# Attention scores in float32r, two heads side by side in TensorE's row halves

## The reference

```python
h = emb[x]
Q, K, V = (heads(wq, bq), heads(wk, bk), heads(wv, bv))
score = jnp.einsum('bhsd,bhtd->bhst', Q, K) / jnp.sqrt(jnp.float32(D_K))
attn = jax.nn.softmax(score, axis=-1)
o = jnp.einsum('bhst,bhtd->bhsd', attn, V)
o = o.transpose(0, 2, 1, 3).reshape(B, S, D_MODEL)
return o @ wo + bo
```

## Time and profile before

| | us |
|---|---|
| median of 3 runs | 3909.69 (3908.48 to 3920.23) |
| profiled execution | 3908.45 |
| its span, first to last instruction | 3906.5 |
| TensorE busy | 3578.8 (92%) |
| VectorE busy | 2969.2 (76%) |
| ScalarE busy | 2761.6 (71%) |
| GpSimd busy | 1451.6 (37%) |

### The profile page before, as it was taken

The page is one execution under the profiler, slowest core; times in us unless marked ns, Lnnn a source line. Parts: engine busy times, 40 slices in busy tenths (PEclk is TensorE's granted clock), DMA queues, the critical chain, the costliest instruction groups (busy, mean ns, idle before and its releaser), DMA issues. The chain is left out here.

```text
span 3906.5 us, 64143 instructions
## 1 busy us (share of the span) xinstructions
PE 3578.8 (92%) x20577; PEld 1947.6 (50%) x20577; DVE 2969.2 (76%) x3944; ACT 2761.6 (71%) x3830; POOL 1451.6 (37%) x1284
## 2 busy tenths in 40 slices
PE   7699999999999999945899999999999999998688
PEld 4223333223323333222577777777777677777454
DVE  5799999889989999423588888888888888889122
ACT  2246666666666666822788999889898999988133
POOL 3000000000000000000577877777777887779000
PEclk9789999999999999977999999999999999999799
DMA  5510101010101000033011111111111111111412
GB/s 140 144 47 4 42 4 42 4 42 9 38 12 33 26 19 4 5 107 114 28 44 55 60 55 55 50 49 61 55 59 57 55 55 56 52 47 55 147 70 75
DMA packets 122134, 202.72 MB, mean 52 GB/s; under 512 B 25696, under 2 KB 68736, under 8 KB 121888
## 3 DMA queue, kind: packets, MB, share of 16 engines
q1 hardware_dynamic: 101264, 173.97, 14.0%
q10 hardware_dynamic: 19088, 21.24, 1.8%
q0 software_dynamic: 1536, 4.20, 0.7%
HBM read 148.23 MB, written 50.72 MB: 51 GB/s over the span
## 5 line engine op out<-in xcount | busy, mean ns | idle before, releaser
L1047 POOL TENSOR_TENSOR m_g<-m_hs,m_cb 128x512 f32<-128x512 f32 x1024 | 1295.4, 1279 | 375.3 <-DVE m_hs L1322 371.7
L661 DVE TENSOR_REDUCE a_mx<-a_ps_m 128x1 f32<-128x512 f32 x2048 | 1311.3, 685 | 158.1 <-PE a_ps_m L520 140.5
L632 ACT ACTIVATE a_probs<-a_ps_s 128x1024 f32<-128x1024 f32 x1024 | 995.0, 1020 | 466.9 <-PE a_ps_s L557 466.3
L1322 DVE TENSOR_TENSOR_SCAN m_hs<-m_da,m_carry,m_ps_x 128x512 f32<-128x512 f32 x768 | 967.6, 1274 | 178.8 <-PE m_ps_x L1118 157.6
L1248 ACT ACTIVATE m_da<-m_delta,m_a_cur 128x512 f32<-128x512 f32 x1024 | 735.7, 719 | 102.1 <-DVE m_hs L1322 101.3
L520 PE MATMUL a_ps_m<-a_k,a_q 112*128 112x512 bf16 x2048 | 732.6, 394 | 42.2 <-DMA a_q<-q_scr 26.7
L1233 ACT ACTIVATE m_bu<-m_dut,m_bt 128x512 f32<-128x512 f32 x1024 | 732.2, 715 | 0.2
L1118 PEld LDWEIGHTS m_ps_x<-m_ident,m_bu 128*128 128x128 f32 x4096 | 489.7, 143 | 389.3 <-issue 306.9
L1118 PE MATMUL m_ps_x<-m_ident,m_bu 128*128 128x128 f32 x4096 | 630.5, 277 | 45.2 <-DVE m_hs L1322 31.3
L1130 PE MATMUL m_ps_y<-m_ident,m_g 128*128 128x128 f32 x4096 | 619.8, 274 | 12.3 <-POOL m_g L1047 12.3
L557 PE MATMUL a_ps_s<-a_q,a_k 115*128 115x512 bf16 (+1 forms) x2048 | 612.1, 381 | 1.4
(11 more groups left out here) (154 smaller groups left out, 2311.3 us busy)
## 6 DMA issues: line engine op xcount, KB each, us to landing
m_cb<-c_scr SPq DMA_DIRECT2D x128, 512.0 KB, 3.7
y_scr<-m_ysb SPq DMA_DIRECT2D x16, 1024.0 KB, 6.6
ffn_y<-y_scr SPq DMA_DIRECT2D x16, 1024.0 KB, 10.3
a_k<-k_scr SPq DMA_DIRECT2D x224, 64.0 KB, 2.2
a_q<-q_scr SPq DMA_DIRECT2D x224, 64.0 KB, 2.6
m_xn<-xn_scr SPq DMA_DIRECT2D x16, 512.0 KB, 4.9
q_scr<-p_partsq SPq DMA_DIRECT2D x24, 256.0 KB, 2.4
k_scr<-p_partsk SPq DMA_DIRECT2D x24, 256.0 KB, 2.6
```

Source lines behind the costliest of these rows:

```text
L632: nc.scalar.activation(probs[:, t % 2, 2 * half:2 * half + 2], ps_s[half][:, :, :], ACT.Exp, scale=float(DK) ** -0.5).then_inc(exped, 1)
L661: nc.vector.reduce_max(mx[:, i // NC, i % NC:i % NC + 1], bank(i), AX.X).then_inc(m_maxed, 1)
L1047: nc.gpsimd.tensor_tensor(g[:, t % NG], hs[:, t % NHS], cb[:, quarter % 2, n % CQ], ALU.mult).then_inc(g_ok, 1)
L1322: nc.vector.tensor_tensor_scan(hs[:, t % NHS, rev], da[:, t % NDA, rev], ps_x[:, t % NX, rev], carry[:, n, i:i + 1] if p else 0.0, ALU.mul ...
```

## The change

Scores are computed from float32r, with two parts of q and k (`PARTS = 2`) and three part products in 48 rows (50 with the maximum). Two heads lie in partitions 0 to 63 and 64 to 127 of `k_st` and `q_st`. ScalarE writes the high part and VectorE the low part of the projection.

In `attention`, step `t` is four items. Each item is one turned product (heads in the order 1, 0, 3, 2) and one maximum product in the other half of the rows. The turned products go round three banks (`SR = 3`) and each exponential reads one bank. The maximum products go round four banks (`MR = 4`) and each maximum on VectorE reads two. The value products are those of step `t - 2` (`LAG = 2`), behind the second item, and `probs` has four buffers (`PR = 4`). The maximum products run 84 items ahead: 64 and `4 * EARLY = 20`, one chunk and five sixteenths. The negative maximum of the next chunk is transposed at item 54 of 64 (`NEG`) and takes a turn of the three banks; ScalarE copies it twice, GpSimd makes the low part (`low`), and SP writes four transfers. At the start, 20 maximum products come first and then the 64 weight transpositions, each followed by one. The loads of a group are 24 transfers of 128 KB. A group's four chunks are written out on TensorE and no longer looped.

```diff
-PARTS = 3
-
-Q_PART = [0, 0, 1, 1, 0, 2, 1]
-K_PART = [0, 1, 0, 1, 2, 0, 2]
+HP = HG // 2
+PARTS = 2
+
+Q_PART = [0, 0, 1]
+K_PART = [0, 1, 0]
...
+        parts = [sb(f"p_parts{n}", [P, 2, PARTS, KD, CH], F32R) for n in "qk"]
...
+                        act.wait_ge(stored[a][buf], ONE + (n - buf) * 8 * PARTS)
                         for m in range(KD):
-                            nc.scalar.activation(full[a][:, m], ps_qk[a][:, m], ACT.Identity,
-                                                 bias=b_col[a][:, m:m + 1]).then_inc(full_ok[a], 1)
+                            nc.scalar.activation(parts[a][:, buf, 0, m], ps_qk[a][:, m], ACT.Identity,
+                                                 bias=b_col[a][:, m:m + 1]).then_inc(high_ok[a], 1)

...
-                        dve.wait_ge(full_ok[a], ONE + KD * n + KD)
...
-                        nc.vector.tensor_copy(part[0], full[a][:, :, :]).then_inc(step, 1)
...
-                        nc.vector.tensor_tensor(part[2], rest[:, :, :], part[1], ALU.subtract).then_inc(parts_ok[a], 1)
-                        dve.wait_ge(parts_ok[a], ONE + n + 1)
+                        for m in range(KD):
+                            dve.wait_ge(high_ok[a], ONE + KD * n + m + 1)
+                            last = nc.vector.scalar_tensor_tensor(
+                                out=parts[a][:, buf, 1, m], in0=ps_qk[a][:, m], scalar=b_col[a][:, m:m + 1],
+                                in1=parts[a][:, buf, 0, m].bitcast(FP32), op0=ALU.add, op1=ALU.subtract)
+                        last.then_inc(parts_ok[a], 1)
...
-        k_st = sb("a_k", [P, 2, HG, S], BF16)
-        q_st = sb("a_q", [P, 2, NC, HG, CH], BF16)
+        SR, MR, PR, LAG = 3, 4, 4, 2
+        k_st = sb("a_k", [P, 2, HP, S], F32R)
+        q_st = sb("a_q", [P, 2, NC, HP, CH], F32R)
         v_st = sb("a_v", [P, 2, NT, HG, VW], FP32)
...
+        probs = sb("a_probs", [P, PR, HG, CH], FP32)
...
+        BLK = NM * NC
...
-        ps_s = [pb(f"a_ps_s{i}", [P, 2, CH], FP32) for i in range(2)]
-        ps_m = pb("a_ps_m", [P, 3, CH], FP32)
+        neg_col = sb("a_neg_col", [NM, P], FP32)
+        neg_rows = sb("a_neg_rows", [NM, PARTS, P], F32R)
+        ps_s = pb("a_ps_s", [P, SR, CH], FP32)
+        ps_m = pb("a_ps_m", [P, MR, CH], FP32)
...
         w_load, w_clear, w_transpose, w_copy, w_store, w_count, w_copied, w_stored = weight_transposes(
-            nc, sem, sb, ident32, [ps_s[i // 2][:, i % 2] for i in range(4)], *weights)
...
-
-
-        AHEAD = 2
-        NEG = 15
-        ITEMS = BLK + 1
-        def item(i):
+        EARLY = 5
+        ITEMS = HG * NT
+        HEADS = [1, 0, 3, 2]
+        NEG = 54
+        OPS = 2 * (BLK // MR)
+        W_AFTER = BLK + HG * EARLY - w_count
+        W_NEG = w_count - HG * (EARLY - 2)
+        def slot(i):
             return i if i < NEG else i + 1
-        def bank(i):
-            return ps_m[:, item(i) % 3]
-        ps_n = ps_m[0:PARTS * NM, NEG % 3].bitcast(BF16)[:, 0:P]
+        def turned(i):
+            return ps_s[:, slot(i) % SR]
+        def maxed(r, b):
+            return 2 * r + b // 2 + 1
+        ps_n = ps_s[0:NM, NEG % SR, 0:P]
...
-                        dst = q_st[KQ + i:KQ + i + 1, buf, bass.ds(c, 1)].rearrange("a c h (s n) -> a (c h s) n", n=P)
-                        sp.dma_start(dst, neg_rows[i * NM:(i + 1) * NM, :]).then_inc(neg_in, 16)
-                    sp.wait_ge(neg_in, ONE + 16 * PARTS * (m + 1))
+                    for r in range(2):
+                        for i in range(PARTS):
+                            row = r * (P // 2) + KQ + i
+                            dst = q_st[row:row + 1, buf, bass.ds(c, 1)].bitcast(FP32).rearrange("a c h (s n) -> a (c h s) n", n=P)
+                            sp.dma_start(dst, neg_rows[r * NM // 2:(r + 1) * NM // 2, i].bitcast(FP32)).then_inc(neg_in, 16)
+                    sp.wait_ge(neg_in, ONE + 32 * PARTS * (m + 1))
                     sp.nop(nofuse=True)
...
+                def low(m):
+                    pool.wait_ge(neg_h, ONE + m + 1)
                     pool.nop(nofuse=True)
-                    nc.gpsimd.tensor_copy(neg_parts[:, 0], neg[:, :]).then_inc(neg_step, 1)
-                    pool.wait_ge(neg_step, ONE + m * 3 + 1)
-                    nc.gpsimd.tensor_tensor(neg_rest[:, :], neg[:, :], neg_parts[:, 0], ALU.subtract).then_inc(neg_step, 1)
...
+                def max_free(m, i):
+                    r, b = divmod(i, MR)
+                    if r or not isinstance(m, int) or m:
+                        pe.wait_ge(m_maxed, ONE + m * OPS + maxed(r - 1, b))
+                def max_score(buf, c, i):
+                    pair, st, tc, half = i // 32, i // 8 % 4, i // 2 % 4, i % 2
+                    row = half * (P // 2)
+                    nc.tensor.matmul(ps_m[:, i % MR], q_st[row:row + KQ, buf, c, pair, st * P:(st + 1) * P],
+                                     k_st[row:row + KQ, buf, pair, tc * CH:(tc + 1) * CH],
+                                     start=True, stop=True).then_inc(m_scored, 1)
+                def max_blocks(m, buf, c, first, end, loads):
                     for i in range(first, end):
+                        if i % 32 < 2 and loads is not None:
+                            pe.wait_ge(loaded[buf][2 * (i // 32) + i % 2], ONE + loads)
+                        max_free(m, i)
+                        max_score(buf, c, i)
...
+                def turned_free(e, i, with_neg):
+
+                    q = slot(i) - SR
+                    if q >= 0:
+                        if q == NEG and with_neg:
+                            pe.wait_ge(neg_h, ONE + e + 2)
                         else:
+                            pe.wait_ge(exped, ONE + e * ITEMS + (q if q <= NEG else q - 1) + (q != NEG))
+                    elif not isinstance(e, int) or e:
+                        pe.wait_ge(exped, ONE + e * ITEMS + min(0, q + 2))
...
+                def turned_score(buf, c, t, h):
+
+                    row = h % 2 * (P // 2)
+                    nc.tensor.matmul(turned(HG * t + HEADS.index(h)), k_st[row:row + KQM, buf, h // 2, t * P:(t + 1) * P],
+                                     q_st[row:row + KQM, buf, c, h // 2], start=True, stop=True).then_inc(scored, 1)
...
                         last = nc.tensor.matmul(ps_o[h * VW:(h + 1) * VW, :], v_st[:, buf, t, h],
-                                                probs[:, t % 2, h], start=t == 0, stop=t == NT - 1)
+                                                probs[:, t % PR, h], start=t == 0, stop=t == NT - 1)
                     last.then_inc(pv_done, 1)
...
+                    pe.wait_ge(neg_in, ONE + 32 * PARTS * (e + 1))
...
                     for t in range(NT):
-                        maximum()
-                            for i in range(2):
-                                last = nc.tensor.matmul(ps_s[half][:, i], k_st[0:KQM, buf, 2 * half + i, t * P:(t + 1) * P],
-                                                        q_st[0:KQM, buf, bass.ds(c, 1), 2 * half + i].rearrange("p c n -> p (c n)"),
-                                                        start=True, stop=True)
-                                if i == half:
-                                    maximum()
-                        if with_neg and t == 3:
-                            if m_buf is None:
-                                transpose_neg(e + 1, G * NC * BLK + 2)
-                            else:
-                                transpose_neg(e + 1, (e + AHEAD) * BLK + NEG)
-                        maximum()
-                        if t > 0 or v_buf is not None:
-                            pe.wait_ge(exped, ONE + e * NT * 2 + t * 2 + 2)
-                            if t == 1:
-                                pe.wait_ge(o_copied, ONE + e)
-                            values(v_buf if t == 0 else buf, (t - 1) % NT)
-
+                        block, ahead = (first, 1) if t + EARLY < NT else (second, 2)
+                        for j in range(HG):
+                            i = HG * t + j
+                            m = (i + HG * EARLY) % BLK
+                            if i == NEG and with_neg:
+                                pe.wait_ge(exped, ONE + e * ITEMS + NEG - SR + 1)
+                                transpose_neg(e + 1)
+                            if block is not None:
+                                m_buf, m_c = block
+                                if m_buf != buf and m_c == 0 and m % 32 < 2:
+                                    pe.wait_ge(loaded[m_buf][2 * (m // 32) + m % 2], ONE + loads)
+                                max_free(e + ahead, m)
+                            turned_free(e, i, with_neg)
+                            turned_score(buf, c, t, HEADS[j])
+                            if block is not None:
+                                max_score(m_buf, m_c, m)
+                            if j == 1 and (t >= LAG or v_buf is not None):
+                                pe.wait_ge(exped, ONE + e * ITEMS + HG * (t - LAG + 1))
```

(51 more changed lines are left out.)

168 lines of the change are left out of this document (47 added, 121 removed).

## The result

The changed kernel took 3878.4 us (median of six runs, 3866.3 to 3894.6) beside 3910.0 for the kernel before: a ratio of 0.9916 with a 95% interval of 0.9889 to 0.9944. The interval leaves out 1, but the gain is under 1%. The direction was right and the size was not: 32 us came instead of 168. Its profiled execution took 3872.7 (span 3870.8) against 3908.45.

The account below looks back on a forecast made before the run. TensorE's 2.84 us step bounded attention; the ring of three banks would make it 2.43, a chunk 40.2, and attention 1306 against 1455 (-149). With the start's -17, 3908.45 becomes 3742 us, range 3655 to 3830.

Parts of the forecast that it names:

- One pass, row halves side by side, the ring and not an engine decides: Attention's score products: float32r takes one pass, both row halves overlap, and the ring of three banks sets the step.
- VectorE's 2.27: Attention step: two maxima of two banks at a pace of 1.13 take VectorE 2.27 us, lower bound of the step.
- I put a pair at 0.22 (0.30 at most, if two loads of 0.14 do not hide): TensorE in attention: two products in the two row halves, with their float32r weight loads, are issued in 0.22 us.
- the ring's wait: Three score banks: a product waits 1.11 us behind that of three places earlier, 0.47 to the reader, 0.60 and 0.04.
- the forecast's 2.43: Attention step: ring wait 1.11, pair 0.22 and value block 1.10 make 2.43 us, bounds 2.27 and 2.56.
- The chunk's extras, 1.3: Each attention chunk: output copy, two maxima copies, a transposition and the ring's start add 1.3 us, bounds 0.6 and 2.5.
- The chain of the maxima "just fits", charged 0: Chunk's start: transposition, copies and transfers of the maxima take 5.3 us, ten pairs last about 5.7; 0 charged.
- 18 us are left for loop returns and both ends: Attention before the change: what remains of 1455.3 us after thirty chunks (1371) and the last two (67), left unchanged.
- The start, 0.67 an item: Attention's start: 64 weight transpositions, each with a maximum product, 0.67 us each, bounds 0.57 and 0.85, 43 us.
- Stores, 7.6 us uncovered: Attention's start: ScalarE's eight stores of transposed weights, formerly under running maxima, put 7.6 us ahead of the first exponential.
- Rival (e): Attention: the clock falls to half because pairs leave TensorE less busy, a tile about 3.7, +400 us; chance 0.04.
- Rival (b): Attention: the neg chain is late or pairs take 0.30, 41.6 to 43 a chunk, 3787 to 3831; chance 0.18.

Follow-up runs that it names:

- run 2: Changed kernel with exponentials over only 256 of each bank's 512 columns, the other half of the probabilities left at one: 3779.3 us.
- run 3: Changed kernel with each maximum on VectorE reading 256 of each bank's 512 columns, so maxima over half the keys: 3869.7 us.
- run 10: Changed kernel with the column maxima transposed at item 60 of a chunk's 64 instead of 54, 1.5 steps later: 4042.2 us.
- run 5: Changed kernel with attention's start in rounds of four weight transpositions, then four maximum products, instead of one and one in turns: 3870.1 us.
- run 8: Changed kernel, still float32r, with value block in two 256-column blocks, start in rounds of four, unread products in the last steps, stores from SP: 3768.1 us, 0.9636 of before.
- run 1: Changed kernel with two bf16 parts instead of two float32r parts, in the same rows, banks and order: 3749.3 us.
- run 7: Changed kernel with each of the 64 weight transpositions of attention's start issued twice: 3884.6 us.
- run 6: Changed kernel with unread products of the maximum's shape in the other row half during the last 21 steps: 3872.6 us.
- run 4: Changed kernel with each step's value block in two blocks of 256 columns, one behind each two items: 3791.6 us, 0.9688 of before.
- run 9: Changed kernel in bf16 parts, with value block in two 256-column blocks, start in rounds of four, weight stores from SP: 3648.4 us, 0.9321 of before.

## Why the prediction failed, by its own steps

- **One pass, row halves side by side, the ring and not an engine decides**: right, by the pair's two starts and by runs 2 and 3. VectorE's 2.27 is close behind, as run 2 shows.
- **"I put a pair at 0.22 (0.30 at most, if two loads of 0.14 do not hide)"**: the failed step, 92 of the 131 us. The doubt written there was right and its size was not. The two float32r loads of a pair start together and last 0.185 each, beside a pass of 0.21, and a pair takes 0.34. Ahead of the value block it is 0.43 instead of 0.22 and a share of the switch; the ring's wait is 1.18 instead of 1.11, with 0.54 instead of 0.47 to the reader; the block with its switch behind is 1.00 of the 1.10. Together +0.18 a step and 92 us. With bf16 loads the step is 2.39 against the forecast's 2.43. The Trainium skill (TensorE: Matmul & The Clock Gate, Weight-path perf modes) has the fast weight load only for inputs that are not FP32, about twice as fast; 93 against 185 ns agree. By the formula of the Trainium skill (TensorE: Matmul & The Clock Gate, LDWEIGHTS), which goes by columns alone, an estimate is 107 ns for either type; here the measurement decides.
- **The chunk's extras, 1.3**: right in size, 43.17 - 16 x 2.61 = 1.4 (copies of the outputs at 849.44 and 892.61), and in part by luck. The forecast listed ScalarE's operations and the ring; 0.42 of it is the wait for VectorE at the chunk's edge (run 3).
- **The chain of the maxima "just fits", charged 0**: right; run 10 shows how narrowly.
- **"18 us are left for loop returns and both ends"**: misread, at little cost. In the kernel before, two chunks took 52.7 and 54.2 instead of 45.7, where TensorE waited 5.43 (782.37) and 5.86 (1155.32) for something that no row names. These are 15.5 of the 18. The changed kernel has them too, 46.8 and 48.2.
- **The start, 0.67 an item**: wrong. Full items took 1.125 at a clock of 0.50, all 64 together 64.1 us instead of 43. The clock was feared and came; by the forecast's own terms at half the clock (0.22 + 0.43 + 0.25) an item is 0.90. The rest is the order: a maximum product between two transpositions stands alone and pays both changes of shape, and in rounds of four (run 5) the start reaches VectorE's pace at half the clock. Four more us went into a wait for the weights' own load at 163. The wait for the stores was less than allowed for, so 20.5 are left.
- **Stores, 7.6 us uncovered**: right in kind; 5.33 in this order, 8.05 in run 5, none in run 8.
- **Rival (e), the clock**: inside the attention it came true for 8.8 us in the last steps. Two short falls, seen in the stretches from 757 to 762 (0.66) and from 1109 to 1119 (0.50), stand behind waits of 3 us that the kernel before has too.
- **Rival (b)**, pairs of 0.30, came nearest: 3787 to 3831. Its upper end has 43 us a chunk, and 43.2 came. That the measured time lies above the range is for the most part not the pair: it is the start's 20.5, the last steps' 9 and the 6.5 behind the attention, of which the range held little. But 0.34 a pair and 0.43 ahead of the block were beyond the bound all the same, for the bound of an operation that no row showed was taken from a load of another type in another place.

Open is why the clock stays at 0.50 in the start. The kernel before went to 1.00 there, with 112-row products and two transpositions an item; bf16 does not bring that back (0.50 from 170 to 200 in run 1), nor does a second transposition (run 7). Products over more rows were not tried alone. In the last steps the clock held with a partner in the other row half (run 6), but also with shorter steps and none (runs 1, 2 and 4), so what holds it is open there too.

## What to carry to other kernels

When a product's pass is as short as its weight load, price the load by its own type, and look where it is exposed: behind every semaphore wait and from one pair of row halves to the next. In a ring of PSUM banks the sum of latencies decides, so the longest block that goes between two turns of the ring should be cut before any engine is made faster; here edits of order were worth over three times the change (110 us against 32, run 8). Put operations of one shape together, not in turns, so that those of two row halves can run side by side (run 5), and take queue issues off the engine whose first result all wait for.

## What the runs showed of the hardware

- A float32r product of 48 or 50 rows and 512 columns takes one pass; two in the two row halves start 0.00 to 0.01 us apart. Its weight load of 128 columns takes 185 ns, a bf16 one 93 to 98.
- At a granted clock of 0.50 a maximum product alone between two fp32 transpositions takes 0.73 us until the next. Four in a row, in twos over the two row halves, take 1.15 (run 5, 163.80 to 164.95).
- An idle stretch of 3.21 us on TensorE (run 10, ended at 918.22) was followed by a granted clock of 0.50 for some 12 us, though it was busy all the time again.
- From 168 to 227 us in the changed kernel TensorE was busy for 59.00 of 59 us, with maximum products and transpositions in turn, and the granted clock was 0.50 throughout.
- A two-bank maximum takes 1.22 us at a pace of 1.13 to 1.14; exponentials of one bank 0.60 at a pace of 0.49 in bursts of four and 0.51 over 46 (run 9).
